# A four-layer graph network on one core: 24 and 42 source-row gathers ahead of two waits, a table store behind the first dense go, another behind a dense load, one dense half ahead of each listed round

## The reference

```
h = relu(layernorm(x));  x = x + L0(h)   # degree norm: n * (segment_sum((n*h)[dst], src) + n*h)
h = relu(layernorm(x));  x = x + L1(h)   # sum of theta[k] * lap^k(h), four steps over the edges
h = relu(layernorm(x));  x = x + L2(h)   # per edge: relation bases, gate, segment_sum over dst, self loop
h = relu(layernorm(x));  x = x + L3(h)   # ten steps: h = 0.9 * norm*segment_sum((norm*h)[src], dst) + 0.1*h0
```

## Time and profile before

| | us |
|---|---|
| median of 3 runs | 2373.91 |
| lowest, highest | 2371.91, 2374.13 |
| the profiled execution's own time | 2372.29 |
| its span | 2370.5 |
| VectorE busy | 1841.0 (78%) |
| GpSimd busy | 1445.6 (61%) |
| ScalarE busy | 386.6 (16%) |
| TensorE busy | 327.4 (14%) |

### The profile page before, as it was taken

One profiled execution on the slowest core, in us unless ns is written; L12 is line 12 of the kernel. 1 busy time (PEld: TensorE's weight loads), 2 busy tenths in 40 slices (PEclk: granted clock), 3 DMA queues, 4 the chain that ended last, 5 costly groups with the idle time before them and its releaser, 6 DMA issues. The chain is left out here.

```text
span 2370.5 us, 13019 instructions
## 1 busy us (share of the span) xinstructions
PE 327.4 (14%) x2316; PEld 243.1 (10%) x2316; DVE 1841.0 (78%) x3276; ACT 386.6 (16%) x1277; POOL 1445.6 (61%) x1429
## 2 busy tenths in 40 slices
PE   0000000202000000010000002026605640000430
PEld 0000000201000000000000001014403430000430
DVE  8998889898799586988598998999999997143110
ACT  0000002020121011201011210137716741000000
POOL 6666676372577247404677770177677765777775
PEclk9999999999999955555555555557656665555555
DMA  1001103010122106102102221000011002101000
GB/s 21 16 9 21 20 15 123 6 12 6 52 89 65 33 7 219 29 22 79 55 28 75 68 95 55 0 8 9 8 36 36 7 7 70 11 10 36 11 11 7
DMA packets 58029, 88.42 MB, mean 37 GB/s; under 512 B 26485, under 2 KB 49992, under 8 KB 56312
## 3 DMA queue, kind: packets, MB, share of 16 engines
q0 software_dynamic: 44960, 19.03, 5.3%
q1 hardware_dynamic: 7160, 43.31, 4.7%
q10 hardware_dynamic: 5856, 25.60, 2.8%
HBM read 37.41 MB, written 54.81 MB: 39 GB/s over the span
## 5 line engine op out<-in xcount | busy, mean ns | idle before, releaser
L1903 POOL DMA_INDIRECT out<-outs,i_src x196 | 223.7, 1141 | 181.5 <-DVE outs L1624 108.1
L1897 POOL DMA_INDIRECT xd<-in_x,i_dst x196 | 204.9, 1046 | 109.8 <-DVE mf L615 55.1
L1897 POOL DMA_INDIRECT xs<-in_x,i_outS x196 | 196.0, 1000 | 71.5 <-issue 56.4
L615 DVE TENSOR_TENSOR mf<-mf 128x128 f32<-128x128 f32 (+6 forms) x582 | 181.2, 349 | 10.5
L2136 ACT ACTIVATE pay<-pay 128x1248 f32<-128x1248 f32 (+1 forms) x63 | 75.6, 1199 | 564.3 <-DVE pay L1321 553.9
L615 DVE TENSOR_TENSOR pay<-psum,pay 128x512 f32<-128x512 f32 x196 | 130.4, 685 | 16.7 <-ACT pay L2226 14.5
L1648 DVE TENSOR_REDUCE z<-pay 128x512 f32 (+1 forms) x196 | 132.4, 676 | 0.0
L1903 POOL DMA_INDIRECT out<-outs,i_srcX x100 | 104.0, 1040 | 33.1 <-issue 28.3
L2369 PE MATMUL psum<-pay 128*128 128x512 f16 x196 | 102.5, 523 | 151.5 <-ACT pay L2211 98.2
L1903 POOL DMA_INDIRECT out<-z,i_srcX x96 | 94.5, 985 | 40.0 <-DVE z L1648 23.9
L1897 POOL DMA_INDIRECT mf<-l_own_rows,lists x50 | 49.8, 997 | 76.4 <-DVE mf L1423 61.5
(11 more groups left out here) (565 smaller groups left out, 2730.3 us busy)
## 6 DMA issues: line engine op xcount, KB each, us to landing
outs<-in_x ACTq DMA_DIRECT2D x14, 624.0 KB, 7.9
out<-outs ACTq DMA_DIRECT2D x14, 624.0 KB, 2.9
z<-in_x ACTq DMA_DIRECT2D x6, 624.0 KB, 5.5
out<-z ACTq DMA_DIRECT2D x6, 624.0 KB, 3.5
payload_by_dst<-z SPq DMA_DIRECT2D x1, 3234.0 KB, 9.5
sums_by_edge<-z SPq DMA_DIRECT2D x1, 3234.0 KB, 17.3
z<-sums_by_edge SPq DMA_DIRECT2D x1, 3234.0 KB, 13.3
l_first_rows<-mf SPq DMA_DIRECT2D x1, 3234.0 KB, 9.6
```

The source lines that it names most:

```text
L615: return V.tensor_tensor(o, a, b, op)
L1897: G.indirect_dma_start(out=dest(k), out_offset=None, in_=table, in_offset=bass.IndirectOffsetOnAxis(ap=idx[:, k:k + 1], axis=0), bounds_ch ...
L1903: G.indirect_dma_start(out=table, out_offset=bass.IndirectOffsetOnAxis(ap=idx[:, k:k + 1], axis=0), in_=source(k), in_offset=None, bounds_ ...
```

## The change

It sets how many source-row columns GpSimd fetches before each of its two waits (108 in place of 84, then up to 150 in place of 104). It moves the store of `y_dram` in SP's order from behind the first table to ahead of the load of the sums, behind the first `dense_go`, and lets the store of `x2_dram` wait until half 2 has been loaded. ScalarE starts the loads of halves 2 and 3 when VectorE has written the first table and its own copies out of `outs` are done, and no longer waits for the second `dense_go`. Halves 5 and 6 go ahead of the waits for the gathers of the second and third step. The whole diff:

```diff
--- before.py
+++ after.py
@@ -49,7 +49,7 @@
 TAIL_P, TAIL_C = 32, 5
 assert P * DROWS + TAIL_P * TAIL_C == N
 XS_PARTS = ((0, 104), (104, 150), (150, EC))
-ROWS_BEFORE_LIST = 84
+ROWS_BEFORE_LIST, ROWS_BEFORE_SUMS = 108, 150
 IN_FLIGHT = 4
 SENDS_AHEAD = 38
 FILLS_LISTING, FILLS_PLACING, FILLS_TURN = 38, 18, 6
@@ -539,12 +539,14 @@
                 sp.wait_ge(s[lay + "_listed_ready"], 1)
                 by_slots(lay, "own_listed", OWN1, cuts, s[lay + "_listed_stored"])
 
+            by_dst = y_dram.rearrange("(p c) w -> p (c w)", p=P)
+            sp.wait_ge(s["dense_go"], 1)
+            sp.dma_start(by_dst, xd_t[:]).then_inc(s["y_table"], 16)
             sp.wait_ge(s["sums_scattered"], 16 * W0)
             sp.dma_start(z_t[:], by_edge).then_inc(s["sums_in"], 16)
             listed_tables("l1", XSW, XS_PARTS)
-            by_dst = y_dram.rearrange("(p c) w -> p (c w)", p=P)
-            sp.dma_start(by_dst, xd_t[:]).then_inc(s["y_table"], 16)
             sp.wait_ge(s["s2_ready"], 1)
+            sp.wait_ge(s["dense_in0"], 32 * (MIDDLE_HALF // 2) + 32)
             sp.dma_start(x2_dram.rearrange("(p c) w -> p (c w)", p=P), z_t[:, 0:EW]).then_inc(s["s2_stored"], 16)
             sp.wait_ge(s["fits1_set"], 1)
             longest = sp.value_load(fits[0:1, 0:1], min_val=0, max_val=EC)
@@ -1500,16 +1502,14 @@
 
                 l1_step(0, m2)
                 for i in range(1, L1_STEPS - 1):
+                    dense_half(ROUNDS_HALF + i, ROUNDS_IN)
                     dve.wait_ge(s["l1_third_in"], 16 * w2 * i)
                     l1_step(i, m3)
-                    if i == 1:
-                        dense_half(ROUNDS_HALF + 1, ROUNDS_IN)
                 ch = Chain(dve, s["l1c_chain"], base_n + (L1_STEPS - 1) * PER2)
                 ch(tt(home2i[:, 0:w2], own2[:, :, D + 2], away2[:, 0:w2], ALU.add))
                 V.tensor_copy(small[:, 2:3], small[:, 3:4]).then_inc(s["x2c2_ready"], 1)
 
                 V.memset(small[:, 1:2], 0.0).then_inc(s["s_final"], 1)
-                dense_half(ROUNDS_HALF + 2, ROUNDS_IN)
                 dve.wait_ge(s["dense_done"], 2 * LATE_HALF + 1)
                 dve.wait_ge(s["s_final"], 1)
                 V.memset(small[:, 2:3], 0.0).then_inc(s["dense_go"], 1)
@@ -1950,11 +1950,11 @@
             pool.wait_ge(s["pay_stored"], 16)
             pool.wait_ge(s["many_listed"], 2)
             gather(lambda q: M0[:, q, 0:PAYLOAD], pay_dram, edge0, last[P * EC], s["m0_in"], W0)
-            source_rows(ROWS_BEFORE_LIST, XS_PARTS[0][1])
+            source_rows(ROWS_BEFORE_LIST, ROWS_BEFORE_SUMS)
             pool.wait_ge(s["agg_stored"], 16)
             pool.wait_ge(s["sums_ready"], 1)
             scatter(agg_dram, lambda q: T0[:, q, 0:PAYLOAD], edge0, last[P * EC], s["sums_scattered"], W0)
-            source_rows(XS_PARTS[0][1], EC)
+            source_rows(ROWS_BEFORE_SUMS, EC)
             pool.wait_ge(s["l1_zero"], 1)
             pool.wait_ge(s["l1_own_stored"], 16 * len(XS_PARTS))
             gather(lambda k: OWN1[:, k, :], tables["l1", "own"], owni, last[P * EC], s["l1_own_in"], W1)
@@ -2179,7 +2179,8 @@
 
             norm(U, OUT)
             feed(OUT)
-            act.wait_ge(s["dense_go"], 2)
+            act.wait_ge(s["l1_first_ready"], 1)
+            act.wait_ge(s["fed"], feeds[0])
             dense_halves(MIDDLE_HALF, ROUNDS_HALF, MIDDLE_IN)
             norm(Tc, Fc, W1)
             act.wait_ge(s["fits1_set"], 1)
```

## The result

| | before | after |
|---|---|---|
| median, us | 2373.83 (4 runs) | 2316.39 (4 runs) |
| lowest, highest | 2371.91, 2374.13 | 2315.18, 2317.90 |
| the profiled execution's time | 2372.29 | 2316.06 |
| its span | 2370.5 | 2314.3 |

The ratio is 0.9756, with a 95% interval of 0.9744 to 0.9767: 57.4 us less, where 58.1 were forecast. The later set of five runs gave 2316.83 and 0.9757 (0.9744 to 0.9771).

A forecast was written before the change was run, and what follows sets the result against it. VectorE was taken to bound up to about 1940 us, then a GpSimd gather and scatter chain. 19.8 - 2.0 + 17.2 + 21.7 + 1.4 = 58.1 us off 2372.3 gives 2314.2, plus 1.6 for the median 2315.8; range 2310 to 2327.

The forecast's parts named there:

- The source rows: VectorE's wait for source rows before its third part goes whole when 46 columns move earlier: gain 19.8 us.
- The margin before the payload gather: GpSimd's idle time left before the payload gather, once 24 columns move ahead of the list: 3.1 us.
- The one before the sums' scatter: GpSimd's idle time left before the sums' scatter, with 42 columns instead of 20 ahead of it: 23.7 us.
- The tail: VectorE's wait for the 20 KB tail load, issued beside the moved y store: 2.0 us longer, bounds 0 and +9.
- The first rival: The 20 KB tail load waits behind the whole y store, 9 us in place of 2: 2322.8 us, chance 0.14.
- The loads of halves 2 and 3: Issued when ScalarE's last copy ends, they let half 2 start near 904.7, not 921.84: gain 17.2 us, bounds 13 and 19.4.
- The rival of 13: Half 2's loads are not quicker for being earlier and take 11 us: gain 13, time 2320.0 us, chance 0.12.
- no cost: The x2 store, held until half 2 is loaded, starts at 904.7 in place of 898.0 and delays nothing.
- The own and first rows: Their gathers move 17.8 us earlier, VectorE 35.0; at least 10 us of slack remains, so no new wait.
- The rounds: Halves 5 and 6 before the second and third steps cover the third table's gather, gain 21.7; half 7's load gains 1.4 us.
- all four parts: The forecast's pieces: source rows, y store at first dense go, loads of halves 2 and 3, a half ahead of each round.
- The clock rival: In layer 2's loop TensorE's clock stays at 0.50 and the loop begins to bind: slower, 2386.4 us, chance 0.02.

The follow-up runs named there:

- part 1 alone: Only the source rows move (108 before the first list, up to 150 before the sums), against the kernel before: 2355.97 against 2376.39 us, ratio 0.9917.

## Why the prediction was right

**The source rows.** Forecast 19.8, measured with part 1 alone: 19.8 at half 2 and 20.4 in the time. The margin before the payload gather was right to 0.1 us. The one before the sums' scatter was not (15.87, not 23.7), because the 22 rows were counted at 1.30 each and three took 10.9 together. The Trainium skill ("SBUF — State Buffer", "Who interferes with whom"), named in the prediction as what speaks against the change, says of a VectorE instruction with two SBUF inputs that it contends with a GpSimd instruction that reads SBUF. The rows bear it out in direction: those of 4.33, 1.52 and 5.06 us stand beside VectorE's work on SBUF tiles in all nine traces with rows at this place, and beside a product of the same size with an input in PSUM a row keeps its 1.00. The same section has it that `tensor_tensor` was not seen to stall a DMA; here it does. That VectorE holds GpSimd is read from these rows side by side; no run took the instructions away. The size could have been read ahead of the change. The prediction looked at source rows alone, which took at most 1.12 us, but the trace of the kernel before has a scatter held so near its end:

```profile
1533.63 6.69 DVE L615 TENSOR_TENSOR mf<-mf 128x6272 f16<-128x6272 f32 x1
1534.75 6.43 POOL L1903 DMA_INDIRECT out<-outs,i_src  x1 [0.30 <-issue]
```

The price stayed in slack, as the prediction said it would: the scatter itself is as early as VectorE lets it be. The run with all rows ahead of the scatter shows that a scatter 52 us later would be hidden as well.

**The tail.** Forecast +2.0 between 0 and +9, measured +2.6, and brought back to 0 by moving the store. The first rival (behind the whole store, +9) is out. The 2.0 was a choice between bounds, leaning on a gather held under the load of the sums (by 2.9 us and not 3.2: the 3.21 of the earlier trace rows are its whole idle time, with the 0.3 of issue in it); that it came so near is in part luck. By the rule of the Trainium skill ("DMA: Bandwidth & Descriptors", "Queues, rings and completion order"), that an engine changes between queues after each packet, the prediction had estimated about +1: right in that the 20 KB do not stand behind 3,136, too low by 1.6.

**The loads of halves 2 and 3.** Forecast 17.2 between 13 and 19.4. The gain at the waits is 19.38 - 1.53 = 17.9 less 0.8 more for the table (3.32, not 2.50): 17.0. The rival of 13 is out. What the prediction did not separate is which edit does it: the two stores' absence is worth 8.5 and 7.4, each measured in its own surroundings, the earlier issue 3.4; the three overlap, since they sum to 19.3. It named the x2 store's new wait "no cost"; that is right, and says too little, since without that wait 7.4 of the 17.0 would be lost.

**The own and first rows.** No new wait appeared: their last column starts at 965.8 as forecast (983.5 - 17.8 = 965.7), and VectorE's scans of the first rows start at 991.34 without one.

**The rounds.** Forecast 21.7 + 1.4, measured 58.3 - 34.8 = 23.5 between half 4 (1081.88 before, 1047.09 after) and half 7, of which 1.6 at half 7's load (7.35 to 5.75): right in each. SP's load of `xd` goes out at 1392.61, forecast 1393.

**The sum.** At half 7 VectorE stands 58.3 us earlier, forecast 58.1. Some 0.5 of it is not the change's: VectorE's first product on `xd`, ahead of all four parts, starts at 357.06 after and at 357.60 before. By the terms it is 19.8 - 2.6 + 17.0 + 21.9 + 1.6 = 57.7, each within 0.6 of its forecast. The median of 2316.39 lies 0.6 above the 2315.8, the profiled execution 1.9 above its 2314.2; the 1.6 added for the median was an accident of one set of runs (0.3 after).

The stages behind 1415 us, whose length was to stay, do so within 1.5 us. The clock rival's condition did not arise: in layer 2's loop TensorE's granted clock is 0.66 on average before and 0.63 after, and VectorE takes 352.5 and 353.5 us for it. It would not have been dear either: in the 20 us from 1787, granted 0.50 throughout, TensorE is busy 16.3 us, not the 18.6 forecast, with 109 matmuls, where full stretches of the loop before have 101 to 115 at 0.60 to 0.76. Ahead of the loop the level was 0.50 before (830 to 1585) and 1.00 after, with TensorE busy 31 and 28 us. Of the four timed runs after, two have a mean over the whole execution of 0.849 and 0.847 (2316.06, 2317.90) and two of 0.693 and 0.698 (2316.72, 2315.18), and the time does not follow it.

## What to carry to other kernels

An idle engine ahead of a wait is a place for its own later work, and the gain is the wait that this work's lateness causes elsewhere, not the idle time that it fills: 46 columns, 60 us of GpSimd, brought 19.8. By an estimate from 1.30 us a column, 16 of them would have covered that wait; no run tried it. A large store that nothing needs soon belongs where no load is awaited, and the wait that keeps it there cost nothing here and was worth more than an earlier issue of the load (7.4 against 3.4 here). When single parts are timed alone, look for a wait common to two of them before adding: a delay that is free in one can be paid in full with the other in place.

## What the runs showed of the hardware

- Being issued first does not keep large loads clear of a store on another queue. The loads of halves 2 and 3 end a wait of 1.5 us with both stores out of the way, 8.9 with one issued 1.3 us behind the second of them, and 10.9 with one issued 4.7 us ahead of the first. The stores of 3,136 KB land in 9.5 us, and in 11.0 beside the end of half 3's loads, where the kernel before has 18.3 and 22.2.
- A load of 20 KB issued together with a 3,136 KB store on another queue is 2.6 us later (a wait of 4.26 to 4.29 us in eight traces, 1.64 to 1.77 in five without the store).
- GpSimd's writing of the descriptors of one gather or scatter, about 1.00 us, lasted until 0.9 us after the end of some VectorE work beside it: 4.33 and 5.06 us beside series of 34 scans, 1.52, 2.29 and 2.04 beside a `tensor_tensor` of 128x1564 on SBUF tiles, 6.43 beside one of 128x6272. Beside the 128x1564 with an input in PSUM it took 1.00, and beside a `tensor_reduce` of 6.70 us (1540.36, in the kernel before) 0.98.
